# A hexagonal convolution after a group norm: VectorE without look-ahead, ScalarE's evacuation moved ahead of the next square root, loads five chunks ahead

## What is computed

```python
xp = jnp.pad(gn(x), ((0, 0), (0, 0), (1, 1), (1, 1)))
xp = xp.at[:, :, DST_R, DST_C].set(xp[:, :, SRC_R, SRC_C])   # wrap
up = conv(xp, w_up * UP, b_up)          # stride 2, 5 live taps of 16
left = conv(xp, w_left * LEFT, b_left)
right = conv(xp, w_right * RIGHT, b_right)
out[:, :, 0::2, 0::2] = up
out[:, :, 1::2, 0::2] = left
out[:, :, 1::2, 1::2] = right
return x + out * OUT_MASK
```

## Time and profile before

| | |
|---|---|
| Time, median of 3 runs | 743.91 us (743.77 to 744.04) |
| Time of the profiled execution | 743.65 us |
| Its span, first to last instruction | 741.8 us |
| Mean granted TensorE clock | 0.993 of full speed |
| Busy: PE, DVE, ACT, POOL | 656.3, 667.6, 574.5, 487.5 us |
| Moved by DMA | 269.60 MB, mean 363 GB/s |

### The profile page before, as it was taken

How to read it: one execution, slowest core, us unless ns; L and a number is a source line. 1 busy time by engine, 2 the same in 40 slices (tenths; PEclk the granted TensorE clock), 3 DMA queues, 4 the chain that set the end, 5 groups by cost and what they waited for, 6 DMA issues and landing times.

```text
span 741.8 us, 35919 instructions
## 1 busy us (share of the span) xinstructions
PE 656.3 (88%) x15484; PEld 602.5 (81%) x15484; DVE 667.6 (90%) x1793; ACT 574.5 (77%) x1235; POOL 487.5 (66%) x1109
## 2 busy tenths in 40 slices
PE   1699999999998898898898988988988988989893
PEld 1589999999887887887887887878878878878883
DVE  4999999999889999999999999999999999999940
ACT  3398888888787787787787877877877877878782
POOL 1178777778567576676675675676766766766784
PEclk9999999999999999999999999999999999999998
DMA  9999999999999999999999999999999999999996
GB/s 275 339 349 380 379 376 372 373 360 364 362 374 378 369 372 373 369 377 371 374 363 376 380 368 374 369 374 369 375 377 364 378 365 378 370 373 374 369 327 229
DMA packets 265017, 269.60 MB, mean 363 GB/s; under 512 B 2640, under 2 KB 264784, under 8 KB 264976
## 3 DMA queue, kind: packets, MB, share of 16 engines
q1 hardware_dynamic: 264976, 269.23, 105.8%
HBM read 135.01 MB, written 134.22 MB: 363 GB/s over the span
## 4 chain that ended last, share of the span: by engine, by line
DMA 70%; DVE 18%; POOL 3%; PE 3%; ACT 2%; SPq 1%; issue 1%; POOLq 0%; ACTq 0%
DMA xs<-in_x 43%; DMA out<-xs 27%; DVE stats L233 9%; DVE tn L281 4%; POOL xs L404 3%; PE bank L462 3%; ACT res L343 1%; ACT tn L320 1%; DVE small L265 1%; DVE rstd L272 1%; SPq L190 1%; DVE nmr L276 0%; DVE small L269 0%; DVE m L246 0%; POOL tn L414 0%
## 5 line engine op out<-in xcount | busy, mean ns | idle before, releaser
L462 PE MATMUL bank<-tn,wts 64*64 64x192 f32 (+1 forms) x15360 | 647.0, 325 | 0.0
L462 PEld LDWEIGHTS bank<-tn,wts 64*64 64x64 f32 x15360 | 593.1, 137 | 34.5
L404 POOL TENSOR_TENSOR xs<-res,xs 128x192 f32<-128x192 f32 (+6 forms) x775 | 387.4, 539 | 71.5 <-ACT res L343 70.9
L233 DVE BATCH_NORM_STATS2 stats<-xs 128x6 f32<-128x512 f32 x512 | 347.2, 691 | 43.2 <-DMA xs<-in_x 43.2
L343 ACT ACTIVATE res<-bank,bias 64x512 f32<-64x512 f32 (+5 forms) x640 | 302.0, 472 | 17.3 <-PE bank L462 7.6
L320 ACT ACTIVATE tn<-xs,nmr,rstd 128x256 f32<-128x256 f32 x511 | 258.9, 591 | 9.2 <-DVE nmr L276 7.7
L414 POOL COPY tn<-tn 128x128 f32<-128x128 f32 (+2 forms) x320 | 97.6, 361 | 168.7 <-ACT tn L320 168.7
L281 DVE TENSOR_SCALAR tn<-xs,rstd,nmr 128x256 f32<-128x256 f32 x513 | 197.2, 454 | 2.3
L314 ACT ACTIVATE std<-var 128x16 f32<-128x16 f32 x64 | 13.8, 216 | 127.4 <-DVE var L254 127.4
L473 PEld LDWEIGHTS bank<-blank 128*128 128x128 f16 x64 | 6.1, 95 | 86.4 <-issue 82.6
L473 PE MATMUL bank<-blank 128*128 128x2 f16 x64 | 11.2, 175 | 67.6 <-POOL tn L414 67.6
(11 more groups left out here) (18 smaller groups left out, 17.0 us busy)
## 6 DMA issues: line engine op xcount, KB each, us to landing
xs<-in_x SPq DMA_DIRECT2D x63, 2048.0 KB, 16.8
out<-xs SPq DMA_DIRECT2D x63, 2048.0 KB, 17.0
xs<-in_x SPq DMA_DIRECT2D x4, 512.0 KB, 7.8
out<-xs SPq DMA_DIRECT2D x2, 1024.0 KB, 5.2
tn<-in_L_conv_w_up SPq DMA_DIRECT2D x1, 256.0 KB, 3.6
tn<-in_L_conv_w_left SPq DMA_DIRECT2D x1, 256.0 KB, 4.0
tn<-in_L_conv_w_right SPq DMA_DIRECT2D x1, 256.0 KB, 5.2
bias<-in_L_conv_b_up SPq DMA_DIRECT2D x2, 0.2 KB, 8.6
```

The source lines that it names most:

```text
L233: last = nc.vector.bn_stats(stats[:, k % 2, 2 * u:2 * u + 2].rearrange("p g a -> p (g a)"), both)
L404: last = nc.gpsimd.tensor_tensor(onto, frm, onto, ALU.add)
L462: last = nc.tensor.matmul(psum[bank + j][to:to + C, at:at + cols], wts[first:first + C, NT * rect[0] + n, :], taps(b, rect, tap, first), s ...
```

## The change

Four things change. DVE takes one chunk at a time: all eight `bn` of chunk k, then `moments(k)`, `norms(k)`, `normalise(k)`, with nothing of chunk k+1 between them; `stats` has one half. ACT's order becomes `root(k)`, `normalise(k)`, `evacuate(k-1)`, where it was `root(k)`, `evacuate(k-2)`, `normalise(k)`; so the banks of chunk k-1 are emptied ahead of `root(k+1)`. SP issues whole loads for chunks 1 to 4 at the start, and load k+5 directly behind store k, where it issued loads up to chunk 7 at the start and load k+7 behind store k. The six small loads of the bias move from SP to the front of ACT's list.

```diff
+AHEAD = 5
...
-        stats = sb("stats", [P, 2, G, 3], F32)
+        stats = sb("stats", [P, G, 3], F32)
...
-            load(1)
-            load(2)
-            for t, b in enumerate((b_up, b_left, b_right)):
-                for h in range(2):
-                    sp.dma_start(bias[C * h:C * h + C, t:t + 1],
-                                 b.rearrange("(o a) -> o a", a=1)).then_inc(b_loaded, 16)
-            for k in range(3, SLOTS):
+            for k in range(1, AHEAD):
                 load(k)
             for k in range(NCHUNK - 1):
                 store(k)
-                if 0 < k < NCHUNK - SLOTS + 1:
-                    sp.wait_ge(stored[(k - 1) % SLOTS], 16 * ((k - 1) // SLOTS + 1))
-                    load(k + SLOTS - 1)
+                n = k + AHEAD
+                if n < NCHUNK:
+                    if n >= SLOTS:
+                        sp.wait_ge(stored[n % SLOTS], 16 * (n // SLOTS))
+                    load(n)
...
             for k in range(1, NCHUNK):
-                moments(k, k + 1)
-                norms(k, k + 1)
+                dve.wait_ge(loaded[k % SLOTS], 16 * (k // SLOTS + 1))
+                bn(k, 0, G // 2)
+                moments(k)
+                norms(k)
                 normalise(k)
-                if k + 1 < NCHUNK:
-                    dve.wait_ge(bn_done, k + 2)
...
+            for t, b in enumerate((b_up, b_left, b_right)):
+                for h in range(2):
+                    act.dma_start(bias[C * h:C * h + C, t:t + 1],
+                                 b.rearrange("(o a) -> o a", a=1)).then_inc(b_loaded, 16)
             act.wait_ge(identity, 1)
...
-            root(1)
-            normalise(1, GD)
             act.wait_ge(b_loaded, 16 * 6)
-            for k in range(LAG, NCHUNK):
+            for k in range(1, NCHUNK):
                 root(k)
+                normalise(k, GD)
                 for j in range(NB):
-                    evacuate(k - LAG, k % 2, j)
-                normalise(k, GD)
-            for k in range(NCHUNK - LAG, NCHUNK):
-                for j in range(NB):
-                    evacuate(k, k % 2, j)
+                    evacuate(k - 1, (k - 1) % 2, j)
+            for j in range(NB):
+                evacuate(NCHUNK - 1, (NCHUNK - 1) % 2, j)
```

More of the change, by code:

```diff
@@ L224, in bn, with moments @@
             def bn(k, u0, u1):
-                if k >= NCHUNK:
-                    return
                 s = k % SLOTS
-                if u0 == 0 and k:
-                    dve.wait_ge(loaded[s], 16 * (k // SLOTS + 1))
                 for u in range(u0, u1):
                     both = view(xs, (s * G + 2 * u) * PIX, [(1, PIX), (PIX, 2)])
-                    last = nc.vector.bn_stats(stats[:, k % 2, 2 * u:2 * u + 2].rearrange("p g a -> p (g a)"), both)
+                    last = nc.vector.bn_stats(stats[:, 2 * u:2 * u + 2].rearrange("p g a -> p (g a)"), both)
                 if u1 == G // 2:
                     last.then_inc(bn_done, 1)
-            def moments(k, ahead):
+            def moments(k):
                 done = STAT_OPS * k
-                own = stats[:, k % 2]
-                nc.vector.stream_shuffle(mate[:].rearrange("p g a -> p (g a)"), own.rearrange("p g a -> p (g a)"),
+                own = stats
+                dve.wait_ge(bn_done, k + 1)
+                nc.vector.stream_shuffle(mate[:].rearrange("p g a -> p (g a)"), own[:].rearrange("p g a -> p (g a)"),
                                          [p ^ 1 for p in range(32)]).then_inc(stat_step, 1)
-                bn(ahead, 0, 1)
                 dve.wait_ge(stat_step, done + 1)
@@ L250, in moments @@
                                                op0=ALU.mult, op1=ALU.mult).then_inc(stat_step, 1)
-                bn(ahead, 1, 2)
                 dve.wait_ge(stat_step, done + 5)
@@ L255, in moments, with norms @@
                                                op0=ALU.add, op1=ALU.add).then_inc(var_ready, 1)
-                bn(ahead, 2, 4)
-            def norms(k, ahead):
+            def norms(k):
                 done = STAT_OPS * k + 5
@@ L262, in norms @@
                 nc.vector.reciprocal(small[:, 0], std[:]).then_inc(stat_step, 1)
-                bn(ahead, 4, 5)
                 dve.wait_ge(stat_step, done + 1)
@@ L266, in norms @@
                                                op0=ALU.mult, op1=ALU.mult).then_inc(stat_step, 1)
-                bn(ahead, 5, 6)
                 dve.wait_ge(stat_step, done + 2)
                 nc.vector.tensor_tensor(small[:, 2], small[:, 1], small[:, 0], ALU.mult).then_inc(stat_step, 1)
-                bn(ahead, 6, 7)
                 dve.wait_ge(stat_step, done + 3)
@@ L273, in norms @@
                                                op0=ALU.add, op1=ALU.mult).then_inc(stat_step, 1)
-                bn(ahead, 7, 8)
                 dve.wait_ge(stat_step, done + 4)
@@ L290, in _ @@
             for n in range(4):
[L291 to L294, removed]
+                dve.wait_ge(quarter[n] if n < 3 else loaded[0], 16)
                 bn(0, QUARTER // 2 * n, QUARTER // 2 * (n + 1))
-            dve.wait_ge(bn_done, 1)
-            moments(0, NCHUNK)
-            norms(0, NCHUNK)
+            moments(0)
+            norms(0)
             normalise(0, GD0)
-            bn(1, 0, G // 2)
-            dve.wait_ge(bn_done, 2)
             for k in range(1, NCHUNK):
-                moments(k, k + 1)
-                norms(k, k + 1)
+                dve.wait_ge(loaded[k % SLOTS], 16 * (k // SLOTS + 1))
+                bn(k, 0, G // 2)
+                moments(k)
+                norms(k)
                 normalise(k)
-                if k + 1 < NCHUNK:
-                    dve.wait_ge(bn_done, k + 2)
         @block.scalar
```

## The result

The changed kernel takes **794.25 us** (median of 4 runs, 793.87 to 795.46) against 743.97 us for the kernel before on the same chip: a ratio of 1.0676, 95% interval 1.066 to 1.0692. It is 6.8% slower, where 8.5% (807 us) was predicted, with a range of 757 to 834 us.

The account below looks back on a forecast made before the run. Transfers bound the kernel before at 11.27 us a chunk; DVE's loop would take over at 12.1 us (9.85 bare plus 2.25 waiting for POOL). 27.4 + 62 x 12.1 + 27.9 = 805.5, plus 1.85 outside the span: 807 us, range 757 to 834.

Parts of the forecast that it names:

- The bare turn: DVE's loop per chunk without waits for POOL: normalise 2.59, eight `bn` 4.96, shuffle to normalise 2.30, sum 9.85 us.
- The wait for POOL: DVE's small instructions between shuffle and normalise wait for ends of POOL's adds: 2.25 us a turn, making 12.1 us.
- 12 adds last 6.05 us and end at N + 7.65: POOL's adds of chunk k-1 trail ACT's evacuation, running from N + 1.6 to N + 7.65.
- N: The time at which ACT's `normalise(k)` ends; DVE and ACT start `normalise(k)` together 4.05 us earlier.
- The ends: Outside the 62 turns: 27.4 us up to chunk 1's normalise, 27.9 us behind A(63).
- A(63): Start of `normalise(63)` on DVE and ACT; from there to the end of the span 27.9 us were forecast.
- rival 2: Adds stretch: POOL is blocked too, adds end 1.5 us later, 13.1 us a turn, 869 us; within a 15% case.
- PE's clock: PE idles 1.95 us a chunk, 1.1 before; should the granted clock fall, this idle time makes it up.
- Rival 3: ACT becomes the bound: its turn 10.6 us bare, 11.3 with waiting; alone 744 to 760 us; within an 18% case.
- 5 us to spare: The load of chunk k+5, issued behind store k, lands 5 us before its `bn` starts; nothing on the path.
- A(1): Start of `normalise(1)` on DVE and ACT, forecast at 27.4 us; 62 turns run from there to A(63).

Follow-up runs that it names:

- the DVE part alone: The kernel before with only VectorE's new order (no look-ahead to the next chunk's `bn`), ScalarE's order and loads as before: 822.46 us, ratio 1.1054.
- the run with all eight `bn` ahead of the reciprocal: The kernel before with ScalarE's new order, and the next chunk's eight `bn` moved ahead of the reciprocal, none inside `norms`: 750.04 us, ratio 1.0088.

## Why the prediction was right, and what it did not see

**The direction and the mechanism.** DVE's own turn took the pace from the transfers, because small instructions that stand alone beside POOL's adds wait for them. The runs show it three ways: the cost vanishes with the adds (746.7), moves to other instructions when the adds move (the DVE part alone), and grows by one more instruction beside the adds but not by one in the quiet.

**The bare turn.** Normalise 2.59, `bn` 4.96, shuffle to normalise 2.30: the trace after has 410.69 - 408.10 = 2.59, then 5.00, and 2.31 without adds.

**The wait for POOL, the one term that was mis-sized.** 2.25 us were predicted, 1.99 measured: 408.10 - 403.81 = 4.29 against 2.30. The step "12 adds last 6.05 us and end at N + 7.65" was off. 6.05 us is their length beside the normalisation of the old order; here they last 5.73 us, as in the tail of before. With N = 408.10 + 4.05 = 412.15 they start at N + 1.6, as predicted, and end at N + 7.3, ahead of `rstd`, which the sum let wait. That makes a turn of 11.88 in place of 12.1 us, and 62 x 0.22 = 13.6 us is the whole of the miss (807.4 against 794.02 us of the profiled execution). That an add lets one small instruction through was right for this kernel; the run with all eight `bn` ahead of the reciprocal shows that it isn't a rule, since there `small` was held over several adds.

**The ends.** From A(63) = 764.23 to the end of the span are 28.0 us, predicted 27.9.

**The harder hold by an exclusive lock** (rival 2) is out. POOL's adds last 5.73 us with the small instructions beside them, and 5.76 us with DVE done. Beside the eight pairs of `normalise` they last 6.24 us (DVE's part alone), 0.5 us more. The Trainium skill ("SBUF — State Buffer", "SBUF: two separate sides") says of the two engines that the one which starts later "fully blocks". The traces agree on DVE's side: each long small instruction ends just behind an add or copy. On POOL's side they show these 0.5 us and no more.

**PE's clock.** It was left open as harmless, and was. Ahead of 39 of 64 chunks PE idles over 1.5 us, mostly 1.7 where 1.95 was forecast; ahead of 22 it idles about 0.45 us, behind a chunk of 11.32 us in part of which the granted clock was at half (1.2 in place of 2.4 GHz). Even then PE is done before POOL's `wrap` releases the next chunk. The mean clock is 0.945 (0.993 before).

**What it did not see.** The prediction costed the parts in the order in which they stand together, and that was right for the sum. It would have been wrong for each part alone, as my expectations were. Rival 3 gave ACT's loop 744 to 760 us "alone"; alone, with the look-ahead inside `norms`, it gives 818.4. "5 us to spare" for the load five chunks ahead is true of the changed kernel only. Measured, there are near 12: issued at 408.07, landed 14.4 us later at 422.5, and wanted two turns after 410.69, at 434.4. With ACT's old order the adds end a turn later, and the same lead costs 49 us. Nor did it see that 11.27 us is the pace of before only from chunk 18 on. The 50.3 us are therefore not 0.6 us in each turn: 27.3 us are lost by the shuffle of chunk 18, where before ran turns of 10.2 us, another 25.9 us from there to chunk 63, and the tail gives 2.9 us back. The sum was not hurt by it, since it counts turns of the changed kernel from A(1) on. The parts' own costs are 78.9 (DVE), 74.8 (ACT) and 48.7 us (transfers), together 202; the whole costs 50.3. Given ACT's new order, DVE's part is a gain of 23 us (818.4 to 795.3), for it clears `norms`.

**Left open.** Why a held instruction is sometimes passed over by several adds, and what decides whether the granted clock falls behind a gap of 1.7 us. The version with all eight `bn` ahead of the reciprocal loses its 6 us against before in two places: 3.7 us by the shuffle of chunk 30, its turns being 10.8 us where before has 10.2 at first, and 2 us from there to the end, half of them in the tail. No run separates the late load from the hold that follows it.

## What to carry to other kernels

Cost an order of work as loops, one per engine: start at one instruction, follow to the same instruction one chunk later, and add what is waited for in between; a work item put into a gap on one engine (look-ahead inside `norms`) is free only while the engine that waits for its end has something else to do in that gap. The lead of a load is to be counted in turns of the slowest loop, from issue over landing to the store that issues the next one; one chunk more or less in any other engine's lag changes what lead is enough. Loads issued ahead at the start also buy turns below the pace of the transfers, so look at the first chunks as well as at the middle. And VectorE's small two-input instructions are cheap only where GpSimd is quiet: put the ones that aren't held (here `bn`) beside GpSimd's work.

## What the runs showed of the hardware

- In the changed kernel, a two-input DVE instruction of 0.17 us that was issued while POOL ran an add or a copy ended 0.02 to 0.04 us behind the end of one (433 of 433 that lasted over 0.23 us) and lasted up to 0.66 us. The eight instructions of `normalise`, with `xs` as their one large input, were lengthened too (4.16 us beside adds, 2.59 bare).
- BATCH_NORM_STATS2 (0.68 to 0.73 us), the reciprocal (0.25 us) and the shuffle (0.20 to 0.21 us) showed no such growth, and POOL's 12 adds last 5.73 us beside small ones and 5.76 us without.
- A held instruction was not always let through at the next end of an add: with all eight `bn` ahead of the reciprocal, `small` lasted up to 2.09 us.
- An extra instruction of 0.08 us ahead of such a wait cost nothing beyond the spread (794.61 against 794.25 us).
- The granted clock fell to half in 22 of the 64 chunks, each time 0.2 to 1.4 us behind the end of an idle gap of 1.7 to 2.0 us. It did not fall behind each such gap: six of 1.7 us lie between 260 and 342 us, all at full speed (first row below). In the kernel before, with gaps of 1.1 us, it stood at full speed from 300 to 400 us. It fell behind the gap that ends at 413.92. PE's windows around it (stretch, length, busy, clock, DMA share, GB/s):

```profile
260.00:342.00 82.00, 70.62 (x1686) 1.00 1.07 353
408.00:413.90 5.90, 4.19 (x134) 1.00 1.09 375
414.50:417.80 3.30, 3.30 (x42) 0.50 1.04 314
418.00:425.00 7.00, 7.00 (x198) 1.00 1.09 368
```
